# Attention heads woven with an order of its own for each engine, all eight pairs written out, and the gathers of expert results spread over the pairs

## The reference

```python
xn = _layernorm(x, axis=-1)
x = x + attn(xn, W_K, W_Q, W_V, W_O) + ffn(xn, Wr, Wg, Wu, Wd)

# attn
K = einsum('bpd,ihd->biph', x, W_K)    # Q, V alike
scores = where(tril, einsum('biph,biqh->biqp', K, Q), NEG_INF)
attn = softmax(scores / sqrt(64), axis=-1)
z = einsum('biph,biqp->biqh', V, attn)
out = einsum('bqf,df->bqd', z_flat, W_O)

# ffn
topk_w, topk_idx = top_k(softmax(x @ Wr), 2)     # weights divided by their sum
hidden = silu(x @ Wg[e]) * (x @ Wu[e])
out = sum over the two experts of cw * (hidden @ Wd[e])
```

## Time and profile before

| | |
|---|---|
| median of three runs | 803.75 us (803.19 to 808.1) |
| the profiled execution | 807.68 us, its span 805.9 us |
| busy share of the span | PE 87%, DVE 80%, ACT 70%, POOL 63% |
| mean granted clock of TensorE | 0.972 of full |

### The profile page before, as it was taken

How to read it: one execution, slowest core, us unless ns; L and a number is a source line. 1 busy time by engine, 2 the same in 40 slices (tenths; PEclk the granted TensorE clock), 3 DMA queues, 4 the chain that set the end, 5 groups by cost and what they waited for, 6 DMA issues and landing times.

```text
span 805.9 us, 15635 instructions
## 1 busy us (share of the span) xinstructions
PE 699.0 (87%) x4241; PEld 564.2 (70%) x4241; DVE 644.3 (80%) x1373; ACT 561.1 (70%) x1311; POOL 509.6 (63%) x517
## 2 busy tenths in 40 slices
PE   4519999888889898989898989898999999988884
PEld 3418999766667776777677777676777777766763
DVE  7875776687868887878888888888888888887772
ACT  4714555477767777778787778787787777777671
POOL 6853444199887565656565656565656665678993
PEclk9959999999999999999999999999999999999997
DMA  7418222134252425243443425161607061626011
GB/s 225 127 36 189 60 60 56 42 79 110 65 127 53 109 54 115 59 101 72 94 86 73 99 67 120 40 131 35 147 12 160 14 148 24 135 49 132 27 27 29
DMA packets 35478, 68.27 MB, mean 85 GB/s; under 512 B 5264, under 2 KB 26096, under 8 KB 31344
## 3 DMA queue, kind: packets, MB, share of 16 engines
q1 hardware_dynamic: 33136, 63.08, 34.4%
q0 software_dynamic: 2304, 4.72, 2.5%
HBM read 12.73 MB, written 4.72 MB: 22 GB/s over the span
## 4 chain that ended last, share of the span: by engine, by line
PE 34%; POOL 25%; issue 20%; DVE 7%; ACT 6%; DMA 5%; SPq 2%; POOLq 1%; ACTq 0%; DVEq 0%
POOL probs L564 16%; PE ps_big L1201 5%; DMA k_st<-k_parts 5%; PE ps_mid L1214 4%; PE ps_z L1231 4%; PE ps_z L1230 4%; POOL k_parts L508 3%; POOL z_lo L569 3%; ACT probs L724 3%; PE ps_big L1147 2%; DVE pT_lo L997 2%; PE ps_z L1168 2%; PE ps_z L1169 2%; PE ps_big L1148 2%; PE ps_big L1149 2%
## 5 line engine op out<-in xcount | busy, mean ns | idle before, releaser
L564 POOL TENSOR_TENSOR probs<-probs,rden 128x128 f32<-128x128 f32 (+7 forms) x256 | 298.8, 1167 | 187.7 <-DVE rden L984 186.3
L997 DVE TENSOR_TENSOR pT_lo<-ps_mid,pT_hi 128x512 fp32r<-128x512 f32 (+3 forms) x384 | 201.0, 551 | 42.3 <-ACT pT_hi L739 40.2
L739 ACT ACTIVATE pT_hi<-ps_mid 128x512 fp32r<-128x512 f32 (+3 forms) x384 | 174.6, 491 | 71.2 <-PE ps_mid L1214 69.3
L1201 PE MATMUL ps_big<-k_st,q_st 128*128 128x512 f32 (+2 forms) x768 | 218.5, 386 | 0.0
L1214 PE MATMUL ps_mid<-ident,probs 128*128 128x128 f32 x1152 | 177.0, 279 | 36.8 <-DVE pT_lo L997 25.3
L724 ACT ACTIVATE probs<-ps_big,neg_max 128x128 f32<-128x128 f32 (+7 forms) x256 | 190.2, 743 | 15.0 <-DVE neg_max L979 14.0
L979 DVE TENSOR_REDUCE neg_max<-ps_big 128x1 f32<-128x128 f32 (+7 forms) x256 | 191.2, 747 | 1.6 <-PE ps_big L1201 1.0
L1214 PEld LDWEIGHTS ps_mid<-ident,probs 128*128 128x128 f32 x1152 | 133.6, 141 | 80.6 <-DVE pT_lo L997 40.0
L1230 PE MATMUL ps_z<-pT_hi,v_st 128*128 128x512 f32 (+2 forms) x384 | 132.3, 352 | 0.0
L1231 PE MATMUL ps_z<-pT_lo,v_st 128*128 128x512 f32 (+2 forms) x384 | 129.1, 350 | 0.0
L1201 PEld LDWEIGHTS ps_big<-k_st,q_st 128*128 128x128 f32 x768 | 118.3, 194 | 1.0
(11 more groups left out here) (193 smaller groups left out, 1130.1 us busy)
## 6 DMA issues: line engine op xcount, KB each, us to landing
k_st<-k_parts SPq DMA_DIRECT2D x64, 512.0 KB
q_st<-q_parts SPq DMA_DIRECT2D x64, 256.0 KB
y_dram<-y_sb SPq DMA_DIRECT2D x40, 64.0 KB
raw_gu<-in_L_ffn_Wg_dram SPq DMA_DIRECT2D x9, 176.0 KB, 2.3
raw_gu<-in_L_ffn_Wu_dram SPq DMA_DIRECT2D x9, 176.0 KB, 2.6
raw_d<-in_L_ffn_Wd_dram SPq DMA_DIRECT2D x9, 128.0 KB, 2.6
res<-in_L_attn_x_dram SPq DMA_DIRECT2D x4, 256.0 KB, 3.7
xn_dram<-xn SPq DMA_DIRECT2D x4, 256.0 KB, 2.7
```

Of the source, the lines that this page charges most:

```text
L564: pool.tensor_tensor(rows, rows, col.to_broadcast([P, width]), ALU.mult).then_inc(normed, 1)
L739: nc.scalar.activation(pT_hi[j][buf][:, g * TPB:g * TPB + tiles, (i % TPB) * P:(i % TPB + 1) * P], ps_mid[:, bank, 0:tiles * P].rearrange( ...
L997: nc.vector.tensor_tensor(pT_lo[j][buf][:, kt, q], ps_mid[:, bank, 0:tiles * P].rearrange("p (t q) -> p t q", t=tiles), pT_hi[j][buf][:, k ...
L1201: ins = nc.tensor.matmul(ps_big[:, n % 2, c0:c1], w, k_st[half][h][:, part, c0 - off:c1 - off], start=part == 0 and not masked, stop=part ...
```

## The change

**Units.** A half is still 16 units, but a long unit of one head now stands beside a short one of the other, in `UNITS`: (0, 7), (1, 0), (0, 6), (1, 1), ... with 1152 columns in every two. Units at odd places have at most 512 columns and so leave the second bank of `ps_big[:, 1]` free: it becomes a second bank for z (`z_bank`).

**V products.** They go in eight jobs a half (`JOBS`) of 256 columns each instead of four of 512; the tiles of `pT_hi` and `pT_lo` now lie in one array each, two areas in turn, and the blank tile above the diagonal is one that all jobs share.

**Orders.** Each of PE, ACT, DVE and POOL has a written order of its own for a half, with marks for what belongs to the half before (-) or after (+). In it M is a small product, T a group of turns, S the scores of a unit and V a piece of a V job. A half's first unit is now 1024 columns wide, and S stands four units ahead of T. The small products come as wqkv, k1, q0, k0, v1, q1, t1, o1, v0, o0, t0, wo. SyncE's stack is the same: q when the last q part is there (now q1), then k when the last k part is there (now k0). The loop is gone; all pairs are written out.

**Gathers.** A pair has four (`fetch_y` at every eighth scaling, `add_y` five later), into `yg[k]` with k from 0 to 3.

```diff
-        AHEAD = 3
-        ORDER = [0, 1, 2, 3, 4, 5, 7, 6]
+        UNITS = [(0, 7), (1, 0), (0, 6), (1, 1), (0, 5), (1, 2), (0, 4), (1, 3),
+                 (1, 4), (0, 3), (1, 5), (0, 2), (1, 6), (0, 1), (1, 7), (0, 0)]
+        JOBS = [(0, 3), (1, 0), (0, 2), (1, 1), (1, 2), (0, 1), (1, 3), (0, 0)]
+        ZS = [(0, 1), (1, 0), (1, 1), (0, 0)]
...
-        PROJ_SLOT = {"wqkv": 1, "q0": 2, "q1": 3, "k0": 4, "k1": 6, "v0": 7, "v1": 9, "t0": 11, "t1": 12, "wo": 14}
-        PV_SLOTS = [[(5, 0, 4)], [(8, 0, 3), (9, 3, 4), (10, 4, 8)]]
+        PE_ORDER = read("""
+            Mwqkv T15.0- S4 T0.0 T0.1 Mk1 V6.0- S5 T1.0 Mq0 S6 T2.0 T2.1 V6.1- S7 V6.2- Mk0 T3.0 V7.0- S8 T4.0
+            T4.1 Mv1 S9 V0.0 T5.0 S10 Mq1 T6.0 S11 V0.1 T6.1 V0.2 Mt1 T7.0 S12 V1.0 T8.0 V2.0 T8.1 Mo1- V2.1
...
+        MISC_ORDER = ["wqkv", "k1", "q0", "k0", "v1", "q1", "t1", "o1", "v0", "o0", "t0", "wo"]
...
             def stack(p, b):
 
-                k_q1, k_k1 = (1, 3) if b == 1 else (11, 13)
-                before = p if b == 1 else p - 1
-
-                wait(sp, *part_done(before, k_q1))
+                before, made = (p, 0) if b == 1 else (p - 1, 1)
+                wait(sp, *part_done(before, made, last_of("q", before)))
...
-                wait(sp, *part_done(before, k_k1))
+                wait(sp, *part_done(before, made, last_of("k", before)))
...
+            def gather_y(p, s):
+
+                if s % 8 == 0:
+                    fetch_y(p, s // 8)
+                if s % 8 == 5:
+                    add_y(p, s // 8)
...
+                dst = z_bank[job % 2][:, (m % 2) * 2 * P:(m % 2 + 1) * 2 * P]
                 for kt in range(k0, k1):
...
+                    t = pT_tile(job, kt, 0)
+                    at = slice(t, t + 2) if kt < tiles - 1 else slice(0, t + 2, t + 1)
+                    nc.tensor.matmul(dst, w, pT_hi[:, at, :], start=kt == 0, stop=False, skip_group_check=True)
+                    ins = nc.tensor.matmul(dst, w, pT_lo[:, at, :], start=False, stop=kt == tiles - 1, skip_group_check=True)
...
-            iteration(0, True, False)
-            with pe.Fori(1, PAIRS - 1) as p:
-                iteration(p, False, False)
-            iteration(PAIRS - 1, False, True)
+            for p in range(-1, PAIRS + 1):
+                iteration(p)
```

More of the change, by code:

```diff
@@ L299, in bank_read @@
[L299 to L314, removed]
-                    events.append((SUM_SLOT[j], ("zz", (b, j))))
-                    events.append((OUT_SLOT[j], ("o", (b, j))))
-                    if last and b >= 0:
-                        events.append((OUT_SLOT[j] + TURN_LAG[b], ("turn", (b, j))))
-                for at, event in events:
-                    if at + b * UPH >= -1 and not (b < 0 and first):
-                        plan[at + b * UPH].append(event)
-            return plan
@@ L438, in iteration @@
                 if not last:
[L439 removed]
+                    wait(sp, proj_filled, proj_count(p, 0, "wo"))
                     load_o(p + 1)
                     stack(p + 1, 0)
[L443 to L446 removed]
+            for p in range(PAIRS):
+                iteration(p, p == PAIRS - 1)
             for b, j in TURNS:
@@ L1061, in _ @@
+            for p in range(-1, PAIRS + 1):
+                iteration(p)
+            for j in BLOCKS:
+                add_x(1, j)
         @block.tensor
@@ L1217, in probs_v, with turn_probs @@
-            def probs_v(p, b, h, j, k0, k1):
-                if k0 == 0:
-                    pe.wait_ge(pT_split, group_count(p, b * UPH + h * QT + last_unit(j)))
-                    wait(pe, z_summed, z_count(p, b, h, j) - 1)
-                if k0 == 0 and h == 0 and j == BLOCKS[0]:
-                    k = 17 if b == 0 else 7
-                    pe.wait_ge(*part_done(p if b else p - 1, k))
-                tiles = TPB * (j + 1)
-                buf = (2 * b + h) % PT_BUFS[j]
+            def turn_probs(p, n, g):
+                i = UNITS[n % UPH][1]
+                if g == 0:
+                    pe.wait_ge(normed, unit_count(p, n))
+                count = group_count(p, n) - i // TPB + g
+                bank = group_bank(n, g)
+                wait(pe, pT_split, count - 2)
+                for c in range(min(TPB, i + 1 - g * TPB)):
+                    kt = g * TPB + c
+                    ins = nc.tensor.transpose(ps_mid[:, bank, c * P:(c + 1) * P], probs[n % 4][:, kt * P:(kt + 1) * P], ident[:])
+                ins.then_inc(t_ready, 1)
@@ new lines, in probs_v @@
+            def probs_v(p, b, job, k0, k1):
+                h, m = JOBS[job]
+                if k0 == 0:
+                    pe.wait_ge(pT_split, group_count(p, b * UPH + last_unit(job)))
+                    if job % 4 < 2:
+                        wait(pe, z_summed, z_count(p, b, 2 * (job // 4) + job % 2) - 2)
+                if k0 == 0 and job == 0:
+                    before = p if b else p - 1
+                    pe.wait_ge(*part_done(before, 1 - b, last_of("t", before)))
+                tiles = 2 * m + 2
+                dst = z_bank[job % 2][:, (m % 2) * 2 * P:(m % 2 + 1) * 2 * P]
@@ L1313 @@
+            for p in range(-1, PAIRS + 1):
+                iteration(p)
+            for j in BLOCKS:
+                turn_sum(1, j)
 _INS = ["L0_attn_x", "L0_attn_W_K", "L0_attn_W_Q", "L0_attn_W_V", "L0_attn_W_O",
```

515 lines of the change are left out of this document (236 added, 279 removed).

## The result

The changed kernel takes **865.72 us** (median of 4 runs, 863.37 to 866.97), the kernel before in the same job 804.35 us (803.19 to 808.1): ratio 1.0748, 95% interval 1.0704 to 1.0792. Its profiled execution has a span of 864.3 us. I had forecast 824 and a range of 784 to 848: the sign was right, the loss 61 us where I had 20, and the time lies outside the range.

What follows compares the result with a forecast made beforehand. The q and k stacking DMAs, back to back behind q1, were to pace each half: 20.9 + 1.3 + 1.0 + 18.0 = 41.2 us. 157.5 + 37.5 + 14 x 41.2 + 54.5 = 826.3, +20.4 on the span; 824 us, range 784 to 848.

Steps and rivals of the forecast that it cites:

- The clock, 1.0 a half: PE after standing for the stack: granted clock falls in most halves, costing 1.0 us a half, at most 1.7.
- the one half here that waited longest agrees: Kernel before, PE at 744.86: after a 0.95 us wait the clock stayed full; after the supposed longest, 1.11, it fell.
- The fixed part of the moving, 1.9: q and k DMAs: 1.9 us beside 14.4 us of moving, so 16.3 from q's issue to the first score product.
- my upper value of 17.2: Upper bound from q's issue to the next first score product: 14.4 + 2.5 us and something for gathers.
- The ends: First half 37.5 us against 34.3 before; last half with the closing chain 54.5 against 61.0.
- The section up to q1, 20.9 + 1.3 + 1.75: First score product to q's issue: 20.9 us of PE streaming, 1.3 of waits, 1.75 from q1's streaming to q's issue.
- The stand, 3 to 5 us: PE before each half's first score product: arrives 3 to 5 us before its data, some 60 us in 15 halves.
- Gathers and loop: POOL rises from 47.4 to 55 us a pair, costing nothing in the middle; loop branch 0 to 1 us, taken 0.
- (3): Rival, slower still: today's waits and the clock's fall in full, half 44.4 us, total 869; chance 0.13.
- its halfway case: Slower rival with half of its excess: 846 us in all; the slower rival's chance is 0.13.
- (2): Rival, faster: the stack doesn't pace, PE's order decides, half 36.4 us, total 755, by the median 753; chance 0.18.
- the two issues were to take 8.7 us together: Sign on SyncE's queue: issues of q and k touch, 8.7 us in one run.

Runs made afterwards that it cites:

- the filled kernel: Changed kernel with 22 extra products of 512 columns, results unused, ahead of PE's wait for the stack: 830.31 us, ratio 1.0316.
- its better order: Changed kernel with small products and k subtractions reordered for q0, q1, k0, k1, and the gathers' multiplications and additions later on GpSimd: 755.01 us, ratio 0.9417.
- two repairs: Changed kernel with SyncE issuing k before q, 865.16 us; with GpSimd's k0 subtraction ahead of its unit 6 scaling, 859.32; with both, 777.59.
- k ready first: Changed kernel with SyncE issuing k before q and GpSimd's k0 subtraction ahead of its unit 6 scaling: 777.59 us, ratio 0.9671.
- the kernel with fewer bytes: Changed kernel without the low parts of k in the second copy from the third half on, 2.62 MB for 3.15: 813.69 us, ratio 1.0145.

## Why the prediction went wrong

The sum was 157.5 + 37.5 + 14 x 41.2 + 54.5 = 826.3; the span is 864.3. The first half measured 41.6 (+4.1), fourteen halves 43.28 (+2.1 each, 29), the last 59.2 (+4.7). The mechanism, the stack moved as one behind q1 with PE standing before it, is what the runs show; the failure is in the sizes of terms, above all of the clock.

- **The clock, 1.0 a half.** This is the step that failed most. It is 2.3 a half and 1.6 in the last: 34.7 us in all by the filled kernel, where I had 14. My upper bound, 1.7, was too low as well: I had taken it from one stretch of 3.5 us at 0.55 and then put 1.0, supposing that part of the fall would land in waits. But the section behind the stand is just the one in which PE is busy without a gap (25.51 of 25.60 us), so all of it lands on work. I also misread the kernel before. The 1.11 us at 234.03 were not its longest wait for the stack, and "the one half here that waited longest agrees" was wrong: behind the longest, 1.31 us, the clock stayed full.

```profile
314.20 0.23 PE L1198 MATMUL ps_big<-causal_bf,ident_bf 128*128 128x128 bf16 x1 [1.31 <-DMA k_st<-k_parts]
...
314.20:317.70 3.50, 3.04 (x22) 2.74 (x22) 1.84 (x6) 1.99 (x6) 1.69 (x2) 1.00 0.00 0
```

- **The fixed part of the moving, 1.9.** Moving took 14.7 us of full DMA work, forecast 14.4, at 230 GB/s in the middle of it; beside it stand 2.8 us. k alone had shown 2.5 (from the earlier trace rows), and I shortened it for a slow start "that a full queue hides". The full queue hid nothing: in the changed kernel the first 1.6 us lose 1.1 of full work, and in the kernel before k alone loses 1.1 in its first 2.4 us too. From q's issue it is 17.5 us instead of 16.3, above my upper value of 17.2: 1.2 a half, 17 to 18 us.
- **The ends.** The first half is 41.6 us against 37.5. 0.5 of that is the chain (16.8), and 3.6 lie ahead of q's issue (24.8 us against 21.2), where the granted clock was 0.79 on average and 0.50 from 162 to 170 us; I had 1 us for it. The last half is 59.2 against 54.5. 1.6 are the clock behind the stand; the closing chain from ACT's first copy of z (849.57) takes 14.7 us, counted 13.5, and its six output products are 0.4 to 0.6 us apart, where the kernel before had 0.2 to 0.3. The remaining 1.9 lie in what follows the last scores, which I haven't traced.
- **The section up to q1, 20.9 + 1.3 + 1.75** = 23.95: measured 23.5 at full clock. So the half is off by +1.3 (clock), +1.2 (chain) and -0.45 (this section): +2.1. The section counted from the order, a row's price for each product and 1.3 us of waits was right within 2%; how it parts into streaming and waits the busy time doesn't show.
- **The stand, 3 to 5 us:** 5.7. PE arrives at 452.2, 13.3 us after q1's streaming ended (count 12.6); the longer chain is most of the difference.
- **Gathers and loop:** nothing in the middle, nothing for the loop. The loop was right. Gathers cost little here, as GpSimd's lateness with k0 was covered by q1's (K0 ahead of them and of N6 brought 6 us); no run of the changed kernel leaves them alone out of K0's way. Once the order of the small products is mended their place costs 15 us. "Under every other engine, so nothing in the middle" was the wrong reason: an engine busy for 59% still delayed the part on which everything waited.
- **Rivals.** (3), the slower one, had the clock in full and today's waits, 869; its halfway case 846. The total came near it, but with waits at my value and the excess in the chain and the ends. (2) was wrong for this kernel and right for its better order: without the stand the weave runs at 35.85 us a half and 755 us in all, where I had put 36.4, and 753 by the median. That the totals agree so well is partly luck, since that kernel also has another order of small products than the one I counted. One of the signs I had named missed too: the two issues were to take 8.7 us together and took 9.8.

What I did not see was that k0's part was as late as q1's. It didn't enter the sum, but it decides what mends the kernel.

## What to carry to other kernels

When several transfers release one wait, follow each one's source to the instruction that makes it ready, through every engine's queue, before choosing their order: here two repairs were worth nothing and 6 us alone, and 88 together. A stand can cost its own length and then a low clock on the dense work behind it (5.7 and 2.3 us here); shortening it to 1.9 us on average gave back the clock too, in all halves but one. A rewritten order should be judged after the transfers it strings together are apart again: the weave was 7.5% slower or 6% faster than the kernel before, by where five small products, GpSimd's two subtractions for k and a gather's two operations stood.

## What the runs showed of the hardware

- Copies inside SBUF of 64 partitions each, eight DMAs on one queue, moved 219 GB/s (421 to 429 us, kernel before) to 230 GB/s (444 to 454 us, changed kernel) with all 16 engines full. Eight behind one another needed 2.8 us beside that. Taking 0.52 MB away at the same number of packets saved 2.7 us.
- After stands of 5.1 to 6.2 us the first two score products took 1.22 us in all 15 halves of the changed kernel (row at 457.90, clock 0.50 behind it). After stands of 0.6 to 2.5 us they took 0.73 in the kernels with q0 q1 k0 k1 and with k ready first, and the clock stayed full behind 29 of these 30 stands; behind one of 1.8 us it was 0.76 over 7 us. After stands of 2.5 to 3.5 us it stayed full in four cases of 14 and fell in ten, in one run (the kernel with fewer bytes). In the kernel before it fell after 1.11 us and not after 1.31. The length of the stand alone doesn't decide.
- SyncE's four issues of k, full size, take 5.6 us when q has already landed or hasn't been issued (5.63 at 437.53), and 6.3 to 7.1 right behind q's (6.68 at 443.63).
